# Two-batch attention and expert layer on one core: the second batch's first token group moved into the first batch's closing stage, the last batch's paging moved up by one pair of tiles, and one rank product per tile

## The reference, cut to what matters

```python
def attention(x):                       # x already layer-normed once
    xn = layernorm(x) * gamma + beta
    q, k, v = xn @ w_q.T, xn @ w_k.T, xn @ w_v.T      # 4 heads
    qn, kn = rmsnorm(q, q_gamma) / 8, rmsnorm(k, k_gamma)
    return heads(softmax(qn @ kn.T) @ v) @ w_o.T + b_o

def experts(x):                         # x already layer-normed once
    chosen = argmax(x @ gate_w.T)       # one of 8
    return x + x @ expert_w[chosen].T

x = x + layernorm(attention(layernorm(x)))
x = x + layernorm(experts(layernorm(x)))
```

## Time and profile before

| | us |
|---|---|
| median of three runs | 762.37 |
| profiled execution, its own time | 765.08 |
| its span, first to last instruction | 763.4 |
| PE busy with products | 656.3 (86%) |
| DVE busy | 607.0 (80%) |
| ACT busy | 538.4 (71%) |
| POOL busy | 271.9 (36%) |
| mean granted clock of TensorE | 0.93 |

### The profile page before, as it was taken

How to read it: one execution, slowest core, us unless ns; L and a number is a source line. 1 busy time by engine, 2 the same in 40 slices (tenths; PEclk the granted TensorE clock), 3 DMA queues, 4 the chain that set the end, 5 groups by cost and what they waited for, 6 DMA issues and landing times.

```text
span 763.4 us, 22051 instructions
## 1 busy us (share of the span) xinstructions
PE 656.3 (86%) x8914; PEld 447.4 (59%) x8914; DVE 607.0 (80%) x1169; ACT 538.4 (71%) x866; POOL 271.9 (36%) x454
## 2 busy tenths in 40 slices
PE   4988878999999999867999899999999998706882
PEld 2666544566666656755766556666666567505772
DVE  4799978878887888896887777888887888963884
ACT  3278788888888878582677988888888785713552
POOL 2245565232332322000555622323323220071775
PEclk9589999999999999996898899999999999956997
DMA  7910006997979878121000178879798781024551
GB/s 251 270 37 1 1 17 113 169 162 142 166 144 163 154 144 151 57 69 44 29 29 22 45 133 156 161 141 167 145 163 153 141 153 58 3 96 135 175 164 44
DMA packets 53815, 87.13 MB, mean 114 GB/s; under 512 B 6608, under 2 KB 23250, under 8 KB 53460
## 3 DMA queue, kind: packets, MB, share of 16 engines
q0 software_dynamic: 34848, 65.61, 44.7%
q1 hardware_dynamic: 18020, 18.03, 8.4%
q10 hardware_dynamic: 848, 2.10, 0.8%
HBM read 14.82 MB, written 14.79 MB: 39 GB/s over the span
## 4 chain that ended last, share of the span: by engine, by line
PE 50%; DVE 22%; DMA 10%; ACT 8%; issue 7%; POOL 1%; SPq 0%; POOLq 0%; DVEq 0%; ACTq 0%
PE banks L1300 13%; PE banks L1154 12%; DVE e_l L941 6%; PE banks L1318 5%; DMA e_h<-e_f 5%; PE banks L1319 5%; PE banks L1206 4%; PE banks L1320 4%; DMA e_x<-x_all 4%; ACT e_f L574 2%; DVE x_all L993 1%; PE banks L1191 1%; PE banks L1422 1%; PE banks L1209 1%; ACT x_all L574 1%
## 5 line engine op out<-in xcount | busy, mean ns | idle before, releaser
L941 DVE TENSOR_TENSOR e_l<-e_f,e_h 128x1024 f16<-128x1024 f32 x172 | 207.7, 1230 | 40.5 <-DMA e_h<-e_f 37.5
L574 ACT ACTIVATE e_f<-banks,nbias,c_ 128x1024 f32<-128x1024 f32 x172 | 199.0, 1200 | 44.6 <-PE banks L1300 44.6
L1300 PE MATMUL banks<-q_T,k_T 128*128 128x512 f16 (+1 forms) x1024 | 204.5, 384 | 4.8 <-DVE e_l L807 3.2
L1320 PE MATMUL banks<-v_mm,e_l 128*128 128x65 f16 x2048 | 201.8, 191 | 0.0
L1320 PEld LDWEIGHTS banks<-v_mm,e_l 128*128 128x128 f16 x2048 | 189.6, 99 | 0.0
L1318 PEld LDWEIGHTS banks<-v_mm,e_h 128*128 128x128 f16 x1376 | 126.0, 96 | 44.2 <-issue 24.9
L1318 PE MATMUL banks<-v_mm,e_h 128*128 128x65 f16 x1376 | 136.7, 193 | 9.2 <-DVE e_l L941 4.3
L412 POOL DMA_DIRECT2D e_h<-e_f x148 | 78.5, 530 | 175.7 <-ACT e_f L574 170.1
L1319 PE MATMUL banks<-v_mm,e_h 128*128 128x64 f16 x1376 | 136.2, 195 | 0.0
L1319 PEld LDWEIGHTS banks<-v_mm,e_h 128*128 128x128 f16 x1376 | 127.2, 97 | 0.0
L941 DVE TENSOR_TENSOR e_l<-x_all,e_x 128x1024 f16<-128x1024 f32 x84 | 101.7, 1227 | 21.2 <-DMA e_x<-x_all 17.7
(11 more groups left out here) (268 smaller groups left out, 1237.4 us busy)
## 6 DMA issues: line engine op xcount, KB each, us to landing
e_h<-e_f POOLq DMA_DIRECT2D x148, 256.0 KB, 3.9
e_x<-x_all POOLq DMA_DIRECT2D x70, 256.0 KB, 4.0
x_all<-x SPq DMA_DIRECT2D x12, 512.0 KB, 4.4
rows_d<-e_x SPq DMA_DIRECT2D x1, 5180.0 KB, 24.4
k_T<-rows_d SPq DMA_DIRECT2D x20, 259.0 KB, 3.1
attn_x<-weT ACTq DMA_DIRECT2D x1, 2048.0 KB, 7.6
q_T<-wqkvT SPq DMA_DIRECT2D x1, 768.0 KB, 6.2
out<-k_T POOLq DMA_INDIRECT x40, 2.7
```

The lines of the kernel that those rows point to most:

```text
L574: act.activation(whole[s % ALL % NEF], ps_S[s % ALL % 3], ACT.Exp, bias=bias_of(h, k // NT), scale=CESC).then_inc(s_E, 1)
L941: dve.tensor_tensor(low[s % ALL % NLO], whole[s % ALL % NEF], high[s % ALL % NHI], ALU.subtract).then_inc(s_El, 1)
L1300: ins = pe.matmul(ps_S[s % ALL % 3][:, c * BANK:(c + 1) * BANK], k_T[rows, 1 - c if cross else c, h * N + j * P:h * N + (j + 1) * P], q_T[ ...
L1320: ins = pe.matmul(o, low[s % ALL % NLO][:, at], v[:, 0:DH + 1], start=False, stop=j == NT - 1, skip_group_check=True)
```

## The change

On the boundary between the batches, `group_stats`, `root`, `group_normal`, `group_T`, `high_y` and `low_y` of the second batch's first group move into the first batch's closing stage: DVE does the statistics at the third pair from the end, the normalising at the second from the end and `low_y` at the last. `page(0)` moves behind `normal_qk` of the second batch's first tile, and `ranks(0)` behind its `project`. The wait for all gate scores before that `project` is relaxed to 14 of 16, and the full wait stands before the second half of the projection. In the last batch `page(p)` and, for all but the last pass, `ranks(p)` come one pair earlier. Inside `page` the last instruction that the scatters need is `rowat`, the table has a semaphore of its own. POOL names all tokens before the first scatter. In `ranks`, the products with a tile's `hot` into each later tile and into the total become one product that writes all of them.

Constants, the banks of the ranks, and POOL at the end of a batch:

```diff
-    GATE, PAGE = 5, 21
+    GATE, PAGE = 5, 18
...
-        ps_R = bank(6)[:, D:D + MT * NE].rearrange("p (t e) -> p t e", e=NE)
-        ps_C = bank(6)[:, D + MT * NE:D + (MT + 1) * NE]
+        ps_R = bank(6)[:, D:D + (MT + 1) * NE].rearrange("p (t e) -> p t e", e=NE)
...
-                for p, (pb, ga, gb) in enumerate(PASSES):
-                    if pb == b:
-                        for gi in range(ga, gb):
-                            name_tokens(b, gi)
-                        if b == NB - 1:
-                            for i in range(ga * TG, gb * TG):
-                                scatter_tile(b, i)
+                for gi in range(NG):
+                    name_tokens(b, gi)
+                if b == NB - 1:
+                    for i in range(NT):
+                        scatter_tile(b, i)
```

ACT, in the closing stage, pair i:

```diff
                     y_squares(i)
                     y_root(i)
+                    if i == NP - 2 and b + 1 < NB:
+                        root((b + 1) * NG)
+                    if i == NP - 1 and b + 1 < NB:
+                        high_y((b + 1) * NG)
```

DVE, in the projection (tile n), inside `page(p)`, and in the closing stage (pair i):

```diff
                         normal_qk(n, t)
+                        if first and t == 0:
+                            for p, (pb, ga, gb) in enumerate(PASSES):
+                                if pb == b - 1 and gb == NG:
+                                    page(p)
...
                     dve.scalar_tensor_tensor(out=w_, in0=g_, scalar=float(P), in1=r_, op0=ALU.mult, op1=ALU.add).then_inc(s_pg, 1)
+                    dve.tensor_tensor(tcmp[:, :, :], spread(chunk_id[:, :], 2, NE), spread(i1[0:1, :], 1, NSL), ALU.is_ge).then_inc(s_tab, 1)
                     dve.wait_ge(s_pg, n + 15)
                     dve.tensor_tensor(w_, w_, hot[:, 0:nt, :], ALU.mult).then_inc(s_pg, 1)
-                    dve.tensor_tensor(tcmp[:, :, :], spread(chunk_id[:, :], 2, NE), spread(i1[0:1, :], 1, NSL), ALU.is_ge).then_inc(s_pg, 1)
...
                     dve.wait_ge(s_pg, n + 17)
-                    dve.tensor_reduce(tnew[:, :], tcmp[:, :, :], AX.X, ALU.add).then_inc(s_pg, 1)
-                    dve.wait_ge(s_pg, n + 18)
                     dve.tensor_copy(rowat[:, b * NT + ga * TG:b * NT + gb * TG], prowf[:, 0:nt]).then_inc(s_pg, 1)
...
                     residual(i)
                     gate_scores(i)
+                    if i == NP - 2 and b + 1 < NB:
+                        group_normal((b + 1) * NG, 0)
                     x1_variance(i)
+                    if i == NP - 3 and b + 1 < NB:
+                        group_stats((b + 1) * NG, 0)
+                    if i == NP - 1 and b + 1 < NB:
+                        low_y((b + 1) * NG)
                     if i:
                         x1_factors(i - 1)
-                    passes(page, i - 2)
+                    passes(page, i - 1)
                     passes(choose, i)
```

PE, in `project`, in `ranks(p)`, and in the closing stage (`ranks(0)` also stands behind the first `project` of the second batch now):

```diff
+                if n // NT * NT > 0:
+                    pe.wait_ge(s_gs, n // NT * NT)
                 products(ps_VG[t % 2], three(t % TG, wqkv_h, wqkv_l, 2 * D, 3 * D + NE, *y) + [(ones2[:, :], bq2[:, 2 * D:])]).then_inc(s_P, 1)
...
                     for t in range(nt):
-                        for later in range(t + 1, nt):
-                            pe.matmul(ps_R[:, later, :], ones16[:, :], hot[:, t, :], start=False, stop=False, skip_group_check=True)
-                        ins = pe.matmul(ps_C, ones16[:, :], hot[:, t, :], start=False, stop=t == nt - 1, skip_group_check=True)
+                        ins = pe.matmul(ps_R[:, t + 1:nt + 1, :], ones16[:, :], spread(hot[:, t, :], 1, nt - t),
+                                        start=False, stop=t == nt - 1, skip_group_check=True)
...
-                    passes(i - 2)
-                passes(NP - 2)
-                passes(NP - 1)
+                    passes(i - 1)
+                if b + 1 < NB:
+                    pe.wait_ge(s_al, b * NP + NP)
+                    group_T((b + 1) * NG)
+                else:
+                    passes(NP - 1)
```

49 lines of the change are left out of this document (22 added, 27 removed).

## The result

The changed kernel took 759.04 us (median of 13 runs, 756.07 to 760.98) beside 764.88 for the kernel before on the same chip (13 runs): a ratio of 0.9929, 95% interval 0.9909 to 0.9949, so 5.4 us less, 3.9 to 7.0. The forecast of 5.7 us less is a ratio of 0.9926. A run more than 1.5% above the fastest of its kernel counts as a slow one and is left out of a ratio: this concerns two runs of e5b and three of e13, for which the figure over all runs stands beside it.

The account below looks back on a forecast made before the run. PE was taken to bound most, but DVE's chain the batch boundary and DVE then POOL the last batch's end. Boundary 3.4 plus end 2.3 makes 5.7 us off the 762.37 median: 756.7 us, range 753.4 to 760.2.

Parts of the forecast that it names:

- The start of the projection: Batch boundary: the second batch's first projection starts at 346.4 in place of 353.3, 6.9 us earlier.
- `ranks(0)` for nothing: Behind the second batch's first projection: 17 products take 0.55 us, covered by the third projection's 1.28 us wait; cost nothing.
- `page(0)` at 4.1 us: Behind the first tile's `normal_qk`: `page(0)` takes 4.08 us, leaving 4.7 of 6.9 us at the transposes of q and k.
- The price of the clock: Behind PE's waits at the boundary: transposes and next projection at 1.2 GHz, 4.7 for 3.4 us, cost 1.3 more.
- The rest of the stage, "1.5 us either way": Rest of the second batch's projection stage: low-clock spells falling otherwise may be worth 1.5 us either way.
- The end, 2.3 us (2.65 less 0.35): Last batch: sixteenth scatter 2.65 us earlier, less 0.35 for pairs late behind PE's rank products; bounds 1.4 and 2.7.
- the page goes cold: Rival, boundary: longer wait behind `page(0)`, two more tiles at 1.2 GHz; boundary gives 0.8 to 1.3, 759.1 us; chance 0.17.
- The page is hidden: Rival, boundary: clock holds through both waits; boundary gives 4.7 to 6, the end 2.65; 754.4 us; chance 0.11.
- A colder second batch: Rival, second batch's later projection groups: far longer at 1.2 GHz; at 22 us more it takes 765; chance 0.05.
- The start moves and the stage's end doesn't: Rival: something other than PE paces later groups, only the end's part is left; 760.1 us, or up to 762; chance 0.06.

Follow-up runs that it names:

- e5b: Changed kernel with unused products filling TensorE's two waits at the batch boundary; 0.9932 of the kernel before.
- e13: e12 with TensorE's rank products two pairs behind the choice and all table instructions behind the last page; 0.9915 of the kernel before.
- e1: Kernel before with only the rank products folded into one per tile; 0.9994 of the kernel before.
- e4: Changed kernel with `page(0)` one step further back on DVE, behind the first tile's low parts; 0.9954 of the kernel before.
- e5c: The kernel of e5b run again on another chip, beside the unaltered changed kernel; 0.9932 of the kernel before.
- e8: Changed kernel with `ranks(0)` ahead of the second batch's first projection and `page(0)` ahead of the first tile's sums; 0.9959 of the kernel before.
- e7: Changed kernel with the table's instructions of all passes gathered behind the last page; 0.9979 of the kernel before.
- e12: e5b with more unused products, in five other waits of TensorE; 0.9939 of the kernel before.
- e3: Changed kernel with pages and ranks two pairs behind and names and scatters pass by pass again, so boundary part alone; 0.9958 of the kernel before.
- e2: Kernel before with the end part alone: new `page`, names first, folded ranks, pages and ranks one pair behind; 0.9955 of the kernel before.
- e6: Changed kernel with PE's rank products put back to two pairs behind the choice; 0.9931 of the kernel before.
- e10: Changed kernel, unaltered, measured again on another chip; 0.9987 of the kernel before.

## Why the prediction was right, step by step

**The start of the projection**, 6.9 us earlier: 7.1 in the profile, shown. The order of DVE's operations came as laid out; `low_y` is at 344.37 where 345.1 was worked out, and the start of PE's transposes at 341.17 for 341.7.

**`ranks(0)` for nothing.** 0.63 us long at 2.4 GHz for the worked-out 0.55, and the wait for `normal_qk` shrank from 1.28 to 0.67 as the cover of it. `normal_qk` of the first tile, 354.10 for 361.85, came 7.2 us earlier counted from there, with the projection. The estimate from columns (1216 at 2.2 a ns) was 0.1 us short for products of 8 to 128 columns. e1 shows that folding the products is worth nothing by itself, within 0.2%.

**`page(0)` at 4.1 us** was mis-sized: 5.1. I had named up to 0.8 for POOL and added nothing, because "it is the same POOL work that now meets `page(0)` and leaves `group_normal` alone". Both halves happened: the page lost 0.9 to POOL's two products (and 0.2 to the new order inside it, 4.26 in e4 for 4.08), and the normalising took 1.39 for 2.18, so the sum for the chain was right: 4.8 us left at the transposes of q and k, for 4.7.

The Trainium skill (SBUF — State Buffer, section "SBUF: two separate sides") says that a VectorE operation in a two-port mode and a GpSimd operation hold the shared ports one at a time, for the whole instruction, and so does a VectorE operation with two inputs in SBUF when the GpSimd operation reads SBUF. In `page(0)` it was L1046 and L1050, with one input each, that ended with POOL's product, at 355.6 and 356.3. Whether those two run in such a mode no run here shows. L1048, with two inputs in SBUF, fell where one product ended and the next began (its record overlaps them by 0.05 and 0.15 us) and took its usual 0.28, so it neither bears the rule out nor speaks against it. The prediction's reading of the rule, longer "by as much as POOL's two products take" (1.35), gave too much; 0.9 is what those two lost.

**The price of the clock was the failed term.** The prediction let "the transposes and the next projection" run at 1.2 GHz, "4.7 in place of 3.4 us, both rows. That is 1.3 more". The place was right, the size not: the row of 4.70 had a clock of 0.65, a mixture, and was used as the price of 1.2 GHz. At 0.50 the projection took 5.70, and each of the two sets of twelve transposes around it 1.2 where e5c has 0.7; together 8.1 us for e5c's 4.9, 3.3 more and not 1.3. ("Some 11 us at 1.2 GHz, 3 us lost" in the rest of the stage came from the same row; at 5.70 for 3.26 it would have been 4.7.) The fifth tile was therefore 1.6 us earlier and not 3.4, even below the bound of 2.1, which had been made from the same row. e5b and e5c take just this spell away and are 3.2 and 2.1 us ahead of after at that tile.

**The rest of the stage, "1.5 us either way", was a gain.** From the fifth to the sixteenth tile's projection the three executions with the old boundary take 52.9, 51.6 and 52.9 us, the five with the new one 50.3, 50.1, 50.1, 51.6 and 50.4: 2.0 less in the mean. In the old ones the spell behind the second inner wait, near 400 us, is 6.9 us long by the granted clock, in all three. Of the nine profiled executions whose second batch starts early and whose inner waits are not filled (these five, e4, e8, e5b, e5c) eight have 3.3 to 3.5 there, and e7 6.9. The waits are the same 1.6 us in both. So the shorter spell goes with the new boundary and is hardly chance, but why it is shorter I haven't shown; e12 shows only that all the spells of the stage together are worth some 6 us at the sixteenth tile. The boundary gave 3.2 us both by e3's time and by the means at the sixteenth tile (87.7 to 84.5), and 2.1 to 3.1 by those at `choose(1)`; 3.4 was forecast. Two errors of 1.8 and 2.0 took each other away: at the fifth tile 1.6 (1.2 by the means) where 3.4 were worked out, and 2.0 behind it where nothing was added. The forecast of this half is right by its sum, and that is luck; its terms were not right.

**The end, 2.3 us (2.65 less 0.35).** 2.55 in after, 2.6 in e2, so the 2.65 were right and the 0.35 were not lost. The last page binds the last four scatters, one wait of 1.17 instead of about 2. What I had not seen: the first scatter waited until 659.01 for ACT's `x1_normal` of pair 3, not for `page(1)`'s `rowat` (657.57). PE's hold for `ranks(1)` (2.19 us, and 1.2 GHz behind it) delayed pair 5, and ACT takes the squares of pair 5 ahead of that row. e6 removes the hold and the first scatter is 1.1 earlier. By the rows of after this cost nothing, since the thirteenth scatter waits 1.17 us for `page(3)` anyway, and DVE, for which the 0.35 were meant, never waited; no pair of runs on one chip tests it.

**The rivals.** Of *the page goes cold* the mechanism is half there (the low clock cost 3.3), but not its price. *The page is hidden* was wrong: both waits of PE came. *A colder second batch*: the clock from the fifth tile on was 0.97 for 0.91, the other way. *The start moves and the stage's end doesn't* was wrong by e3's time and by the means of the marks; it is near to what e4 does, with another place of the page.

## What to carry to other kernels

Price work at the low clock from a row whose granted clock is 0.50 over all its length. A row with a mean clock is a mixture, and both the term and its bound come out too small. A serial block that is moved into a chain comes back at the next consumer down the chain, as in e4. So look for a place where the engine idles ahead of its own input, and read what else runs beside it there. When executions of one kernel differ by 3 us at a mark, compare several executions with the same order, at more than one mark. Ask of every change how it moves the waits of TensorE, not only its work. And measure a gain of under 1% on a second chip: here it was 0.7% and 0.1%.

## What the runs showed of the hardware

- With products whose result nobody uses in its waits of 1.4 to 3.3 us, TensorE's clock stayed at 1.00 (e5b, e5c); 86 of them (112 columns, 52 to 56 ns each) cost nothing in the waits and saved 3.2 us behind them. In the profile of e12 no low spell is left in the 70 us from the first projection to the last.
- An inner wait of the same length (1.5 to 1.6 us) was followed by no low spell (after, at 381.19), by one of 3.0 us (e5c, from 380.48), or by one of 3.5 (before, from 383.81).
- Two tiny VectorE operations (128x8, one input) beside a GpSimd product took 0.66 and 0.58 us for 0.16 and 0.17: each ended when the product did.
- The same kernel took 759.0 us in one place and 778.6 on another chip (after, e10). Of the 25.6 us between the spans of the two profiled executions, 16 lie behind the expert's first product, where engines stand still for up to 6 us at a time for no cause that the profile names.
